# Last expert's part of the first 512 tokens by one-hot products, the other experts' parts combined beside it, MLP weights loaded in halves

## The chip, the cores and the metric

One NeuronCore of one Trainium2 chip runs the whole program; there is no traffic with other cores. The metric is the device time of one execution in microseconds (us). TensorE (PE) multiplies, VectorE (DVE), ScalarE (ACT) and GpSimd (POOL) do elementwise work, SyncE (SP) and POOL issue DMAs; each engine takes its instructions in a fixed order and waits on semaphores.

## The reference, cut to what matters

Two layers on x of shape (2, 1024, 256), fp32. The part around the change is the routed feed-forward of layer 0 and the conditional MLP of layer 1:

```
# L0_ffn: N = 2048 tokens, E = 8 experts, top K = 2, capacity cap = 640 per expert
gates = softmax(top_v)                         # of the two largest logits of a token
exp_batches[e, pos] = x[tok]                   # rows of the tokens that picked expert e
h = exp_batches @ W1;  h = gelu(h_inp) * h_gate;  exp_out = h @ W2
out[tok] = sum over k of gate[tok, k] * exp_out[expert, pos]
x = x + out
# L1_cond, per batch: two picked experts (weighted) and a shared one, hidden width 1024
x1 = sum_e w_e * (gelu(x @ g_e) * (x @ u_e)) @ d_e
```

Layer 0 before it is a conditioned linear layer with causal attention (rotary) and a picked SiLU MLP; layer 1 after it is a minGRU scan, an adapted linear layer and a ternary feed-forward.

## The kernel before, in words

Weights and activations of the large products are split in a high and a low fp32r part, so a product is three matmuls for each 128 of depth: `products` (L932 to L938) issues them at L934, L935 and L936. Tokens stand in the free dimension in 4 chunks of 512 (`CH`), `inH`/`inL` hold the input's two parts, `xT` the residual.

`plan()` writes out by hand the order of the units on every engine (`pe`, `act`, `dve`, `pool`, `sp`); the five programs then walk their lists. A unit's `kind` picks the code, `ready(...)` is the semaphore value at which a unit is done. PSUM banks are handed out in rings (`use`, `bank`), and a matmul waits until what was in its bank has been read.

The experts: `gather` (L1908) fetches 128 rows of an expert's tokens with an indirect DMA, from the scratch `routed_input` in DRAM; `xe` turns them by PE transposes (L1082); `w1` makes 2 halves x 4 blocks x 2 parts of hidden values, with `gelu0` on ACT (L1344), `prod1` on DVE (L1705), `he_hi` on ACT (L1350) and `he_lo` on DVE (L1710); `w2` makes five tiles of output rows, `yrow` copies one to SBUF (L1717) and SP stores it to `expert_output` (L2006). There are four `yrow` buffers, so the copy of tile n waits until the store of tile n - 4 has landed. Beside expert e, `coming_expert(e + 1)` splits the next weights (`wf_hi` L1331 on ACT, `wf_lo` L1907 on POOL) and turns the next rows.

Beside the last expert (7) the first MLP weights are split in 8 pieces: `wm_hi` on ACT (L1369), `wm_lo` on POOL (L1937). They come with one indirect DMA of 3 MB (`ld_mlp`, L1932), issued once the last expert's weights have left the stage buffer. After all 40 output tiles are stored, `fetch` (L1947) gathers for a tile of 128 tokens the two experts' rows, `comb` (L1729, L1731) weighs and adds them, `yt` (L1102) turns the tile, `add` (L1736), `xc_hi` (L1374) and `xc_lo` (L1741) make the MLP's input from it. Four tiles are a chunk. While PE has nothing to do here it runs `spin` matmuls (L950) on constants; their numbers stand in `SPIN`. `early_half` runs the first MLP products (`gu_a`) on the first two tiles of the chunk, so that the products of units 0 to 2 are made in two halves of 256 columns. The other 12 tiles are combined one beside each MLP unit (`combining`).

An MLP unit `gu` is 12 matmuls, followed by `gelu1`, `prod2`, `hm_hi`, `hm_lo`, and two units later `dn` (L1131 to L1133) with 6 matmuls. `split_mlp(1)` splits the second MLP's weights beside units 7 to 14, its low part on DVE (L1722).

```
fetch(0) on POOL: waits for all 40 stores of expert_output and for back_gates
gu(0, 0, 0) on PE: waits for xc_lo of the chunk's last tile and wm_lo(0, 7)
yrow(e, j) on DVE: waits for the store of tile n - 4, then for w2(e, j)
```

Before the experts, routing ends with `inv` (L1074), `slots` (L1334, the token of each slot), then the first gathers, with a spin of 27 matmuls on PE meanwhile; `back_rows`, `back_kept` and `back_gates` on DVE make the rows and gates for the way back.

## Time and profile before

| | |
|---|---|
| median of 3 runs | 999.74 us (998.01 to 1001.44) |
| profiled execution | 1008.6 us |
| its span | 1007.4 us, granted TensorE clock 0.993 in the mean |
| PE busy | 953.5 us (95%) |
| DVE / ACT / POOL busy | 497.4 / 436.1 / 272.2 us |
| moved by DMA | 67.48 MB, mean 67 GB/s |

The profiled execution stands 8.9 us over the median of the runs without a profile. Busy shares are over the whole span; the change touches about 60 us in the middle of it and some 10 us before the experts, so these stretches have to be read by themselves.

### The profile page before, as it was taken

How to read it: one execution, taken by the hardware profiler on the slowest of the kernel's cores; microseconds unless marked ns; L12 is line 12 of the kernel's file. 1: busy time of each engine (PE TensorE's matmuls, PEld its weight loads, DVE VectorE, ACT ScalarE, POOL GpSimd, SP SyncE). 2: the span in 40 equal slices, each digit the busy share in tenths (PEclk: the TensorE clock that was granted, in tenths of full speed). 3: DMA queues.
4: the chain of work that ended last, by engine and by line, in shares of the span. 5: the costliest groups of instructions: out<-in, count | busy, mean ns of one | idle time of the engine just before them, and what ended most of it. 6: DMA issues, size and time to landing. Idle time of an engine off the chain costs nothing.

```text
span 1007.4 us, 13258 instructions
## 1 busy us (share of the span) xinstructions
PE 953.5 (95%) x4952; PEld 783.0 (78%) x4952; DVE 497.4 (49%) x947; ACT 436.1 (43%) x820; POOL 272.2 (27%) x243
## 2 busy tenths in 40 slices
PE   5989999999899999999699999999999999998998
PEld 2667767787589999987587788888888888876786
DVE  5645453566444554544467433333333333688544
ACT  2555564523154444544234334244343342326675
POOL 1333221402256555536452014023041140100000
PEclk9999999999999999999999999999999999999999
DMA  7130001102325444441521300302003003000011
GB/s 261 43 106 21 22 1 64 73 22 84 122 47 125 133 114 133 115 152 35 190 57 39 126 1 1 126 0 110 16 1 126 1 0 126 1 1 1 1 42 43
DMA packets 21648, 67.48 MB, mean 67 GB/s; under 512 B 4497, under 2 KB 11921, under 8 KB 19281
## 3 DMA queue, kind: packets, MB, share of 16 engines
q1 hardware_dynamic: 16592, 39.88, 11.2%
q0 software_dynamic: 4704, 26.49, 9.3%
q8 instruction: 40, 0.66, 0.3%
q10 hardware_dynamic: 288, 0.26, 0.1%
q14 instruction: 24, 0.19, 0.1%
HBM read 55.09 MB, written 9.44 MB: 64 GB/s over the span
## 4 chain that ended last, share of the span: by engine, by line
PE 72%; DVE 12%; ACT 6%; issue 4%; DMA 3%; another core or an unknown queue 1%; SPq 1%; DVEq 0%; ACTq 0%; POOLq 0%
PE banks L934 15%; PE banks L936 14%; PE banks L935 14%; PE banks L1132 4%; PE banks L1133 4%; PE banks L1131 4%; PE banks L1014 3%; PE banks L998 2%; PE banks L1181 1%; PE banks L1180 1%; PE banks L1167 1%; PE banks L1168 1%; PE banks L950 1%; PE banks L1005 1%; DMA expert_output<-y_rows 1%
## 5 line engine op out<-in xcount | busy, mean ns | idle before, releaser
L934 PE MATMUL banks<-input_hi,mlp_hi 128*128 128x512 f32 (+1 forms) x396 | 156.1, 394 | 3.9 <-DVE input_lo L1741 2.4
L936 PE MATMUL banks<-input_hi,mlp_lo 128*128 128x512 f32 (+1 forms) x396 | 155.3, 392 | 0.0
L935 PE MATMUL banks<-input_lo,mlp_hi 128*128 128x512 f32 (+1 forms) x396 | 154.8, 391 | 0.0
L1937 POOL TENSOR_TENSOR mlp_lo<-weight_stage,mlp_hi 128x768 fp32r<-128x768 f32 x40 | 73.6, 1841 | 241.8 <-ACT mlp_hi L1369 241.8
L1384 ACT CAST hidden_hi<-hidden 128x512 fp32r<-128x512 f32 x96 | 59.6, 621 | 176.4 <-DVE hidden L1751 108.0
L1757 DVE TENSOR_TENSOR hidden_lo<-hidden,hidden_hi 128x512 fp32r<-128x512 f32 x96 | 66.5, 693 | 71.3 <-ACT hidden_hi L1384 71.3
L1751 DVE SCALAR_TENSOR_TENSOR hidden<-banks,L_expert_weight,gelu 128x512 f32<-128x512 f32 x64 | 48.0, 751 | 97.6 <-PE banks L936 97.4
L1907 POOL TENSOR_TENSOR ffn_w_lo<-weight_stage,ffn_w_hi 128x512 fp32r<-128x512 f32 x48 | 62.0, 1294 | 109.2 <-ACT ffn_w_hi L1331 109.2
L934 PEld LDWEIGHTS banks<-input_hi,mlp_hi 128*128 128x128 f32 x396 | 75.2, 190 | 20.2 <-issue 4.3
L936 PEld LDWEIGHTS banks<-input_hi,mlp_lo 128*128 128x128 f32 x396 | 75.3, 190 | 16.4
L935 PEld LDWEIGHTS banks<-input_lo,mlp_hi 128*128 128x128 f32 x396 | 75.5, 191 | 16.0
L934 PE MATMUL banks<-expert_in_hi,ffn_w_hi 128*128 128x320 f32 x256 | 82.0, 320 | 3.4 <-DVE hidden L1705 1.8
L1378 ACT ACTIVATE gelu<-banks 128x512 f32<-128x512 f32 x96 | 57.3, 596 | 62.7 <-PE banks L936 62.3
L935 PE MATMUL banks<-expert_in_lo,ffn_w_hi 128*128 128x320 f32 x256 | 80.2, 313 | 0.0
L936 PE MATMUL banks<-expert_in_hi,ffn_w_lo 128*128 128x320 f32 x256 | 80.2, 313 | 0.0
L1132 PE MATMUL banks<-hidden_lo,mlp_hi 128*128 128x512 f32 x192 | 75.4, 392 | 0.0
L1131 PE MATMUL banks<-hidden_hi,mlp_hi 128*128 128x512 f32 x192 | 75.1, 391 | 0.0
L1133 PE MATMUL banks<-hidden_hi,mlp_lo 128*128 128x512 f32 x192 | 75.0, 391 | 0.0
L934 PEld LDWEIGHTS banks<-expert_in_hi,ffn_w_hi 128*128 128x128 f32 x256 | 49.2, 192 | 5.4 <-ACT gelu L1344 2.1
L934 PE MATMUL banks<-ffn_w_hi,expert_hidden_hi 128*128 128x256 f32 x160 | 48.2, 301 | 3.5 <-DVE y_rows L1717 3.0
L1710 DVE TENSOR_TENSOR expert_hidden_lo<-hidden,expert_hidden_hi 128x320 fp32r<-128x320 f32 x64 | 33.9, 530 | 34.0 <-ACT expert_hidden_hi L1350 34.0
L1350 ACT CAST expert_hidden_hi<-hidden 128x320 fp32r<-128x320 f32 x64 | 29.4, 460 | 47.5 <-DVE hidden L1705 47.5
(298 smaller groups left out, 2099.2 us busy)
## 6 DMA issues: line engine op xcount, KB each, us to landing
weight_stage<-in_packF SPq DMA_DIRECT2D x8, 1536.0 KB, 6.9
weight_stage<-in_shared SPq DMA_DIRECT2D x2, 3072.0 KB, 10.9
expert_output<-y_rows SPq DMA_DIRECT2D x40, 128.0 KB
weight_stage<-in_cond_w SPq DMA_DIRECT2D x4, 512.0 KB, 6.4
residual<-in_xT SPq DMA_DIRECT2D x4, 512.0 KB, 10.7
first_half_swapped<-first_half SPq DMA_DIRECT2D x32, 64.0 KB, 2.0
routed_input<-x_rows SPq DMA_DIRECT2D x16, 128.0 KB, 1.8
weight_stage<-in_ffn_w SPq DMA_DIRECT2D x2, 1024.0 KB, 6.8
```

The source lines that it names most:

```text
L934: pe.matmul(o, wh, dh, start=(i == 0), stop=False)
L935: pe.matmul(o, wh, dl, start=False, stop=False)
L936: last = pe.matmul(o, wl, dh, start=False, stop=(i == len(terms) - 1))
L1131: pe.matmul(o, dh[:, i, ms], hiD[r][:, :], start=first, stop=False)
L1132: pe.matmul(o, dh[:, i, ms], loD[r][:, :], start=False, stop=False)
L1133: last = pe.matmul(o, dl[:, i, ms], hiD[r][:, :], start=False, stop=final)
L1378: act.activation(gelu_t[n % 2][:, :], bank(("gu", *key, 0)), ACT.Gelu_apprx_tanh, bias=0.0).then_inc(done)
L1384: act.copy(hiD[n % 4][:, :], prod_t[n % 2][:, :]).then_inc(done)
L1751: dve.scalar_tensor_tensor(prod_t[m % 2][:, :], o, wsel[:, n // 3, n % 3:n % 3 + 1], gelu_t[m % 2][:, :], ALU.mult, ALU.mult).then_inc(done)
L1757: dve.tensor_tensor(loD[m % 4][:, :], prod_t[m % 2][:, :], f(hiD[m % 4][:, :]), ALU.subtract).then_inc(done)
L1907: pool.tensor_tensor(lo, src, f(hi), ALU.subtract).then_inc(done)
L1937: pool.tensor_tensor(wDl[s][:, qs], stage[:, qs], f(wDh[s][:, qs]), ALU.subtract).then_inc(done)
```

## The change

- The output rows of expert 7 for the first 512 tokens no longer go through DRAM. A matrix `hot` (640 slots x 512 tokens, 1 where slot s holds token t) is made by five DVE comparisons beside the `w2` of expert 6. ACT and DVE scale expert 7's output tiles by the slot's gate and split them (`hot_hi`, `hot_lo`), and 20 matmuls of 512 columns sum them straight into the layout of the residual. `hot_add`, `hot_in` and `hot_in_lo` finish the chunk.
- For these tokens `fetch` leaves expert 7 out (its gate is set to 0 and its row to 0), so `fetch`, `comb`, `yt` and `add` of tiles 0 to 3 stand beside expert 7; `fetch` of tile 0 waits for the 35 stores of experts 0 to 6. Tiles 4 to 15 are as before and still wait for all 40, but their steps stand one MLP unit later.
- The gate of each slot of expert 7 is got by way of DRAM: SP writes a table of 2048 gates, one float each, in token order (`gate_table`), and POOL gathers 5 x 128 of them beside expert 2 (`gate_of_slot`). Token numbers count from one, with a row 0 of its own, so that an empty slot is no token's.
- The picked MLP weights are loaded in two halves of 1.5 MB. The first half of MLP 0 is issued beside expert 5, the second where the whole one was; five of the eight split pieces stand beside the `w2` of expert 6, three beside expert 7.
- Gone are the spins of 30 and 7 before the first tiles and the halves of `gu`; a spin of 4 stands before the first `gu`; "slots" goes from 8 to 16, "first rows" from 27 to 13. Some small loads share a semaphore.

POOL from the end of expert 7's weight split on, before (`mlp_lo` is `wm_lo`, `y_first`/`y_second` the fetches of a tile, `in_pack` the MLP load):

```order
L1907 TENSOR_TENSOR ffn_w_lo_173<-weight_stage_52,ffn_w_hi_172 128x512 x2
L1932 DMA weight_stage_52<-in_pack,rows_of_L_cond_63 128x6144
L1937 TENSOR_TENSOR mlp_lo_194<-weight_stage_52,mlp_hi_195 128x768 x8
L1947 DMA y_first_206<-expert_output,route_rows_73 128x256
L1947 DMA y_second_209<-expert_output,route_rows_73 128x256
L1947 DMA y_first_207<-expert_output,route_rows_73 128x256
```

and the same place now:

```order
L2004 TENSOR_TENSOR ffn_w_lo_173<-weight_stage_52,ffn_w_hi_172 128x512 x2
L2035 DMA weight_stage_52<-in_pack_1,rows_of_L_cond_63 128x3072
L2040 TENSOR_TENSOR mlp_lo_202<-weight_stage_52,mlp_hi_203 128x768 x5
L2054 DMA y_first_214<-expert_output,route_rows_73 128x256
L2054 DMA y_second_217<-expert_output,route_rows_73 128x256
L2054 DMA y_first_215<-expert_output,route_rows_73 128x256
L2054 DMA y_second_218<-expert_output,route_rows_73 128x256
L2054 DMA y_first_216<-expert_output,route_rows_73 128x256
L2054 DMA y_second_219<-expert_output,route_rows_73 128x256
L2040 TENSOR_TENSOR mlp_lo_202<-weight_stage_52,mlp_hi_203 128x768
L2054 DMA y_first_214<-expert_output,route_rows_73 128x256
L2054 DMA y_second_217<-expert_output,route_rows_73 128x256
```

Three tiles are now fetched after the fifth piece and the fourth after the sixth. The fourth uses the first one's buffer again, so it waits for that tile's `yt` on PE, and behind it stand two pieces and both halves of MLP 1's load.

DVE at the `w2` of expert 7, now (`last_y_lo` is `hot_lo`, `y_rows` is `yrow`, `residual` is `add` at L1833 and `hot_add` at L1810):

```order
L1806 SCALAR_TENSOR_TENSOR last_y_lo_197<-banks,tiny_71,last_y_hi_196 128x256
L1795 COPY y_rows_187<-banks 128x256
L1806 SCALAR_TENSOR_TENSOR last_y_lo_197<-banks,tiny_71,last_y_hi_196 128x256
L1795 COPY y_rows_188<-banks 128x256
L1833 TENSOR_TENSOR residual_49<-banks,residual_49 128x2x128
L1806 SCALAR_TENSOR_TENSOR last_y_lo_197<-banks,tiny_71,last_y_hi_196 128x256
L1795 COPY y_rows_189<-banks 128x256
L1810 TENSOR_TENSOR residual_49<-banks,residual_49 128x512 x2
L1814 TENSOR_TENSOR input_lo_51<-residual_49,input_hi_50 128x512 x2
```

Where five copies stood alone, each has a `hot_lo` ahead of it, and the chunk's last steps stand behind the last copy, which waits for a store.

The diff, cut to its core:

```
-SPIN = {"first scores": 12, "logits": 5, "slots": 8, "first rows": 27, "first tile": 30, "next tile": 7}
+SPIN = {"first scores": 12, "logits": 5, "slots": 16, "first rows": 13, "first hidden": 4}
...
     def down_expert(e):
         for j in range(ST):
             product("down3", "w2", e, j)
+            if e == G - 1:
+                act.append(("hot_hi", j))
+                dve.append(("hot_lo", j))
             dve.append(("yrow", e, j))
+            if e == G - 2:
+                dve.append(("onehot", j))
+                mlp_piece(j)
...
+    def mlp_piece(q):
+        act.append(("wm_hi", 0, q))
+        pool.append(("wm_lo", 0, q))
+
+    def beside_last_expert():
+        for tt in range(3):
+            pool.append(("fetch", tt))
+        for q in range(ST, PIECES):
+            mlp_piece(q)
+            if q == ST:
+                pool.append(("fetch", 3))
+            yield
+        yield
+        for tt in range(2):
+            dve.append(("comb", tt))
+            yield
+        for tt in range(3):
+            product("turn3", "yt", tt)
+            if tt == 0:
+                dve.append(("comb", 2))
+            dve.append(("add", tt))
+            yield
+        dve.append(("comb", 3))
+        yield
+        yield
+        product("turn3", "yt", 3)
+        dve.append(("add", 3))
+        yield
...
         else:
-            run(weave(expert, split_mlp(0)))
+            run(weave(expert, beside_last_expert()))
...
+    for j in range(ST):
+        pe.append(("hot", j))
+    for k in range(KD):
+        dve.append(("hot_add", k))
+        act.append(("hot_in", k))
+    for k in range(KD):
+        dve.append(("hot_in_lo", k))
+    spin(SPIN["first hidden"], HOT + KD)
...
-    use("first_yt", [(4,), (5,)])
-    for n, _ in enumerate(combine_tiles(0, QT)):
-        if n >= QT // 2 + 1:
-            early_half(n - QT // 2 - 1)
-    pool.append(("ld_mlp", 1))
+    for half in range(2):
+        pool.append(("ld_mlp", 1, half))
...
+            elif kind == "hot":
+                j, = key
+                if j == 0:
+                    for i in range(ST):
+                        pe.wait_ge(*ready("onehot", i))
+                pe.wait_ge(*ready("hot_lo", j))
+                for k in range(KD):
+                    ks = slice(k * P, (k + 1) * P)
+                    pe.matmul(banks[:, HOT + k, :], y7H[:, j, ks], hot[:, j, :], start=(j == 0), stop=False)
+                    last = pe.matmul(banks[:, HOT + k, :], y7L[:, j, ks], hot[:, j, :], start=False, stop=(j == ST - 1))
...
+                dve.tensor_scalar(hot[:, j, :], counting[:, :], slot_number[:, j:j + 1], None, ALU.is_equal).then_inc(done)
...
+            elif kind == "gate_of_slot":
+                pool.iota(counting[:, :], [[1, CH]], base=1, channel_multiplier=0, allow_small_or_imprecise_dtypes=True).then_inc(ramps)
+                pool.wait_ge(ld["gate_table"], 16)
+                for j in range(ST):
...
-                pool.indirect_dma_start(stage[:, 0:PK1], None, A["pack1"], bass.IndirectOffsetOnAxis(ap=dyn1[:, m:m + 1], axis=0)).then_inc(ld["picked_mlp"], 16)
+                pool.indirect_dma_start(stage[:, half * PK1 // 2:(half + 1) * PK1 // 2], None, A[f"pack1_{half}"], bass.IndirectOffsetOnAxis(ap=dyn1[:, m:m + 1], axis=0)).then_inc(ld[f"picked_mlp{half}"], 16)
...
+        sp.wait_ge(*ready("back_gates"))
+        sp.dma_start(gate_rows[1:1 + N, :].rearrange("(n p) a -> p (n a)", p=P), last_gate, allow_slow_non_contiguous=True).then_inc(ld["gate_table"], 16)
```

## Rows read from the trace of the kernel before

**Rows 1.** The page: busy times, and the chain that ended last by engine
```profile
PE 953.5 (95%) x4952; PEld 783.0 (78%) x4952; DVE 497.4 (49%) x947; ACT 436.1 (43%) x820; POOL 272.2 (27%) x243
...
PE 72%; DVE 12%; ACT 6%; issue 4%; DMA 3%; another core or an unknown queue 1%; SPq 1%; DVEq 0%; ACTq 0%; POOLq 0%
```

**Rows 2.** Timeline of PE: start, length, then the idle time before in brackets
```profile
441.60 0.36 PE L934 MATMUL banks<-ffn_w_hi,expert_hidden_hi 128*128 128x256 f32 x1
...
444.43 0.28 PE L936 MATMUL banks<-ffn_w_hi,expert_hidden_lo 128*128 128x256 f32 x1
444.55 0.31 PE L934 MATMUL banks<-expert_in_hi,ffn_w_hi 128*128 128x320 f32 x1
...
448.81 0.31 PE L936 MATMUL banks<-expert_in_hi,ffn_w_lo 128*128 128x320 f32 x1
...
472.08 6.65 PE L950 MATMUL banks<-earlier_token,identity_bf 128*128 128x512 bf16 x30
...
495.39 0.35 PE L934 MATMUL banks<-input_hi,mlp_hi 128*128 128x256 f32 x1 [2.38 <-DVE input_lo L1741]
...
699.79 0.39 PE L935 MATMUL banks<-input_lo,mlp_hi 128*128 128x512 f32 x1
...
704.91 0.39 PE L1133 MATMUL banks<-hidden_hi,mlp_lo 128*128 128x512 f32 x1
```

**Rows 3.** Windows: busy of PE, PEld, DVE, ACT, POOL, granted clock, DMA share, GB/s
```profile
472.00:484.60 12.60, 9.26 (x44) 3.91 (x43) 3.85 (x10) 0.81 (x2) 7.12 (x8) 1.00 0.30 87
484.60:495.40 10.80, 5.12 (x41) 4.78 (x41) 3.11 (x8) 1.41 (x3) 6.35 (x7) 1.00 0.83 315
495.40:500.00 4.60, 4.60 (x26) 4.60 (x27) 1.44 (x2) 2.40 (x4) 0.95 (x1) 0.63 0.67 166
```

**Rows 4.** The chain that ended last, 439 to 479: start, length, what
```profile
439.85 10.17 DMA expert_output<-y_rows
...
475.35 2.82 DMA y_first<-expert_output,route_rows
```

**Rows 5.** Timeline of POOL
```profile
437.65 0.96 POOL L1932 DMA_INDIRECT weight_stage<-in_pack,rows_of_L_cond  x1 [0.81 <-POOL ffn_w_lo L1907]
...
476.61 0.95 POOL L1947 DMA_INDIRECT y_second<-expert_output,route_rows  x1 [0.30 <-issue]
```

**Rows 6.** Timeline of ACT and of DVE beside expert 7
```profile
452.05 0.43 ACT L1344 ACTIVATE gelu<-banks 128x320 f32<-128x320 f32 x1
...
454.19 0.43 ACT L1344 ACTIVATE gelu<-banks 128x320 f32<-128x320 f32 x1
...
450.04 0.42 DVE L1717 COPY y_rows<-banks 128x256 f32<-128x256 f32 x1 [6.24 <-DMA expert_output<-y_rows]
```

**Rows 7.** Groups by line and form: xcount | busy us, mean ns | idle before
```profile
L1937 POOL TENSOR_TENSOR mlp_lo<-weight_stage,mlp_hi 128x768 fp32r<-128x768 f32 x40 | 73.6, 1841 | 241.8 <-ACT mlp_hi L1369 241.8
...
L1563 DVE TENSOR_TENSOR residual<-banks,residual 128x512 f32<-128x512 f32 x8 | 5.5, 692 | 8.0 <-PE banks L936 8.0
L1796 DVE TENSOR_SCALAR below_minus_half<-weight_stage,tiny 128x512 f32<-128x512 f32 x8 | 3.9, 484 | 0.2
...
L1384 ACT CAST hidden_hi<-hidden 128x512 fp32r<-128x512 f32 x96 | 59.6, 621 | 176.4 <-DVE hidden L1751 108.0 <-DVE hidden L1753 68.5
```

**Rows 8.** Timeline of PE and POOL before the first expert
```profile
269.51 1.07 PE L1074 MATMUL banks<-token_at_column,at_low 128*128 128x40 f32 x8 [2.01 <-DVE token_at_column L1651]
270.43 7.69 PE L950 MATMUL banks<-earlier_token,identity_bf 128*128 128x512 bf16 x27
...
280.66 0.38 PE L934 MATMUL banks<-expert_in_hi,ffn_w_hi 128*128 128x320 f32 x1 [0.97 <-issue]
...
273.59 0.94 POOL L1918 DMA_INDIRECT gathered<-routed_input,token_of_slot  x1 [0.30 <-issue]
```

**Rows 9.** DMA queues from 276 to 284: packets, MB, share of 16 engines
```profile
q0 software_dynamic: 315, 0.84, 61.0%
```

**Rows 10.** DMA issues of the whole span: KB each, us to landing
```profile
weight_stage<-in_cond_rep SPq DMA_DIRECT2D x1, 1.0 KB, 2.8
```

186 lines of the change are left out of this document (121 added, 65 removed).

## The prediction

> **What bounds the kernel now.** The page first: PE is busy 95% of the span and makes 72% of the chain that ended last [rows 1], so the kernel is a stream of matmuls, and time can only be won where that stream stops or crawls. The windows by stage show where: between 472.0 and 495.4 us PE's busy time is made of constants' products, transposes and half-width products, with few real columns [rows 3]. The timeline of PE gives the edges of that hole: the last `w2` ends at 472.08, where 30 spins begin, and the first product that needs the whole chunk starts at 495.39 [rows 2]. The chain says what fills it: a store, a gather that takes 2.82 us from issue to landing, and the elementwise steps behind it [rows 4]. A second weak place stands ahead of it: at 439.85 a store of output rows takes 10.17 us, since the 3 MB load was issued at 437.65, and DVE sits idle 6.24 us for it [rows 4, 5, 6]. A third is the wait for the first gathers, which a spin of 27 covers from 270.43 to 278.1, before the first expert product at 280.66 [rows 8].
>
> **The hole before the MLP, before.** Of the first three units' 36 products, the left halves were made inside the hole. Full-width products follow each other by (704.91 - 699.79) / 22 = 0.233 us, 256-wide ones by (444.43 - 441.60) / 24, about 0.119 [rows 2]. Had all been left to do at the end of the hole, it would have cost 36 x (0.233 - 0.119) = 4.1 us more, so the hole's end is worth 495.39 - 4.1 = 491.3.
>
> **The same stretch after the change.** I count from the first `w1` product of expert 7 at 444.55, which the change leaves about where it is.
> - 96 products of `w1` by (448.81 - 444.55) / 29 = 0.147 us [rows 2]: 14.1. Before, a unit took 454.19 - 452.05 = 2.14 us, since ACT had a split piece in each, and DVE had come 6.24 us late [rows 6]. Now three pieces stand here, not eight, and PE is up to two units ahead of them, so PE's own pace counts.
> - four pairs of transposes, 0.3 each: 1.2. They are moved in here, with comb and add, from the hole and hide nothing.
> - 60 products of `w2` by 0.119: 7.2.
> - 20 one-hot products of 512 columns by 0.233: 4.7. The last tile's `hot_hi` and `hot_lo` lie beside the first 16.
> - the tail on the path: `hot_add` 0.69, `hot_in` 0.62, then two `hot_in_lo` of some 0.69 (the row of `hot_add` is the nearest in shape) and the hops [rows 7]: 2.9. The spin of 4 lies inside it.
>
> That is 444.55 + 30.1 = 474.7. I add 1.5 for bank and comb waits (below): 476.2, against 491.3: **-15.1 us**.
>
> What has to hold for it, with what each is behind. The second half load of 1.5 MB is issued at the old place; as 3 MB held the store for 10.17 us, half of it should hold one about 5, so the store issued at 439.85 lands near 445, when the copy that waits for it was due (450.04 less 6.24 is 443.8). The five `wm_lo` of 1.84 us beside `w2` of expert 6 [rows 7] take POOL from about 440 to 450; the three fetches then take 6 issues of 1.25 us (0.95 and 0.30 [rows 5]) to 457.5 and land by 2.8 later: tile 0 at 455, where its comb stands due, tile 2 at 459, some 0.5 late. The fourth fetch waits behind a piece and `yt` of tile 0 and lands near 464, where its comb is due. PE has some 2 us of banks ahead; so 0 to 4 us may be lost here, and I take 1.5. Five comparisons of 0.48 [rows 7] on DVE and five pieces of ACT's beside `w2` of expert 6 fit in its 1.65 us per tile: nothing, and up to 1 if the POOL pieces slow them.
>
> **The first rows.** The spin of 16 instead of 8 runs up to `inv`, where PE sat idle 2.01 us [rows 8]. The third gather is issued at 273.59 and by 2.82 to land is there at 276.4 [rows 4, 8]; at the DMA load of that stretch I say 276.9, and transposes and split add 1.4: first `w1` at 278.3, not 280.66. **-2.3 us.** Here the gate table comes in: five small DVE operations later than the old gates, SP writes 2048 single floats, near 275.5, beside gathers 3 to 5. No row shows such a write. From below, a load of 128 rows of 8 bytes lands in 2.8 us [rows 10]: nothing is lost, and 278.3 stands. From above, gathers of 0.84 MB took 61% of 16 engines over 8 us, 78 us of engines [rows 9], 0.095 for each 1 KB row; 2048 elements at that price are 12 us on 16 engines, and up to that the gathers could come late. An element is nearer to the small row, and the later gathers have 4 us of slack: I take 0 and keep -3.5 to +5. In its own sentence, the rule that speaks against this write: the Trainium skill, DMA: Bandwidth & Descriptors, Rules for kernel authors, says that a strided last dimension "lowers to one descriptor per element" and should be rearranged. With it 2048 descriptors are due; without it, if the short runs were merged, the 2.8 us alone; the forecast takes the first count and a small price.
>
> **The rest.** The half load beside expert 5 is 1.5 MB in front of five gathers and beside five stores; by the same halving a store is held some 5 us, just what the fourth-next copy allows: +0.5, bounds 0 to 3. `gate_of_slot` is six POOL instructions in a gap of over 5 us beside expert 2, ahead of pieces with slack: 0. The combined tiles stand one unit later, so one more unit carries a tile and a DVE split piece together: +0.7. The small loads that now share a semaphore have landed long before its waiters: 0.
>
> Sum: -15.1 - 2.3 + 0.5 + 0.7 = **-16.2 us**. Against the profiled execution of 1008.6 that is 992.4; its 8.9 us over the median stay in both, so I put it on the median: 999.74 - 16.2 = **983.5**.
>
> **The rivals.**
> *The loads of MLP 1 take the store's place.* They are issued right behind the last two pieces: 457.5 + 1.84 + 2.5 for the fourth tile's fetches + 2 x 1.84 is near 466. The store of expert 7's first tile comes near 462: `w1` ends at 459.3, its `w2` 1.4 later, then `hot_lo` and the copy. If POOL is 4 us early or that store late, the fifth copy (it waits for that store) sits until 3 MB are in, near 477.5, and `hot_add` stands behind it, though `hot` ended at 471.6. That gives back some 6 us: 990. For it speaks the row of 10.17 us; against it, POOL's work between. The landing of expert 7's stores also feeds tile 4's comb, due near 484 with some 2 us of slack.
> *The wait moves into expert 7.* The store of expert 6's last tile lands late, fetches start 5 us later, and comb in DVE's fixed order holds `prod1`: 5 us back, 988. The half load speaks against it.
> *The gate table goes ahead of the gathers, at a packet's price.* The 315 packets of the gathers took 78 us, 0.25 us each [rows 9]. One packet for each element makes 2048 x 0.25 / 16 = 32 us in which the third gather waits: `w1` of expert 0 starts near 310, +29 in place of -2.3, in all -15.1 + 29 + 1.2 = +15: 1015, slower. It decides from 0.15 us per element on (19 us). Against it: queues share the engines, and the small load of 128 rows. This is the page's rule at its worst price.
> *No gain.* The hole is mended, but DVE or POOL waits in the new places eat it whole, e.g. both first rivals with a clock that falls, as in the windows, where it stood at 0.63 after the hole [rows 3]. Price: 15 us back, 998 to 1000.
>
> **How the numbers follow.** Forecast as summed 0.66; loads 0.13; wait moved 0.10; no gain 0.04; table 0.04; something better, a clock that stays up, 0.03. A measurement of this kernel tells 0.3%, 3 us, from no change. Faster by more than that: 0.92; same 0.04; slower 0.04. The range takes the bounds of the forecast's own waits and both middle rivals: 978 to 991.
>
> **What would show it.** Right: 20 products on `slot_is_of_token` that follow `w2` without a gap; the first MLP product some 30 to 33 us after the first `w1` product of expert 7, where it was 51 with part of the work done; no DVE wait of over 1 us for a store at expert 7's start; the first `w1` at about 278. Wrong: a copy of `y_rows` waiting for a store ahead of `hot_add` (loads); comb waiting for a fetch by several us in expert 7 (moved); gathers landing late beside the table's write (table). If the gain is under 9 us I have missed a wait; if over 22, a second cost of the old order that I took for hidden.

## The result, and the profile after

The changed kernel takes 1014.12 us (median of 4, 1009.2 to 1015.06) against 1000.51 for the kernel before (4 runs): a ratio of 1.0139 with a 95% interval of 1.0117 to 1.0161. It is **slower by some 13.6 us**; the forecast was 16.2 us faster. A later measurement of both kernels on one chip gave a ratio of 1.0126 [1.0104, 1.0148].

The profiled execution of the changed kernel took 1014.09 us with a span of 1012.8. The kernel before's had 1008.6 and 1007.4. The two spans are thus only 5.4 us apart where the medians are 13.6 apart. That is a finding by itself, and the second profile of the kernel before, below, explains it.

The page of the kernel after, its busy times and the chain that ended last, beside [rows 1]:
```profile
PE 950.8 (94%) x4897; PEld 783.9 (77%) x4897; DVE 515.6 (51%) x965; ACT 438.6 (43%) x823; POOL 282.1 (28%) x253
...
PE 70%; DVE 13%; ACT 7%; issue 5%; DMA 4%; SPq 1%; POOL 0%; DVEq 0%; ACTq 0%
```
PE's share of the chain fell from 72 to 70%, and DVE, ACT, issue and DMA took it. The stalls are in four places: ahead of expert 0, and in experts 2, 6 and 7.

**The first rows.** The timeline of PE and the SyncE queue in the kernel after, the place of [rows 8], then the issues from 274 to 290 with KB each and us to landing:
```profile
271.08 2.98 PE L1004 MATMUL banks<-earlier_token,identity_bf 128*128 128x512 bf16 x13
...
275.83 0.41 PE L1136 MATMUL banks<-identity,gathered 128*128 128x128 f32 x2 [0.83 <-DMA gathered<-routed_input,token_of_slot]
289.40 0.66 PE L1136 MATMUL banks<-identity,gathered 128*128 128x128 f32 x2 [13.16 <-DMA gathered<-routed_input,token_of_slot]
...
291.02 0.61 PE L988 MATMUL banks<-expert_in_hi,ffn_w_hi 128*128 128x320 f32 x1 [0.96 <-issue]
...
274.78 0.38 SPq L2109 DMA_DIRECT2D gate_of_last_expert<-tiny  x1
```
```profile
q1 hardware_dynamic: 2064, 0.01, 7.3%
...
gate_of_last_expert<-tiny SPq DMA_DIRECT2D x1, 8.0 KB, 15.9
```
Read the last two lines together. The write of the gate table is 2048 of the 2064 packets of its queue. They carry 0.01 MB and take only 7.3% of the engines' time, yet the write lands 15.9 us after its issue. The third gather, issued 0.5 us before it, is waited for by PE for 13.16 us. The first `w1` product starts at 291.02, not at 280.66 as before, nor at the forecast's 278.3. It takes 0.61 us instead of 0.38: after the idle 13.16 us the granted clock of the next 5 us is 0.50, where the kernel before had 0.66.

**Experts 6 and 7, up to the MLP.** PE's timeline, where [rows 2] stood:
```profile
453.62 0.69 PE L1136 MATMUL banks<-identity,gathered 128*128 128x128 f32 x2 [2.42 <-DVE expert_in_lo L1776]
...
458.20 0.31 PE L988 MATMUL banks<-expert_in_hi,ffn_w_hi 128*128 128x320 f32 x1
...
472.93 0.41 PE L1156 MATMUL banks<-identity,y_first 128*128 128x128 f32 x2 [2.25 <-DVE y_first L1828]
...
481.17 0.69 PE L1156 MATMUL banks<-identity,y_first 128*128 128x128 f32 x2 [2.87 <-DVE residual L1833]
...
493.55 1.04 PE L1004 MATMUL banks<-earlier_token,identity_bf 128*128 128x512 bf16 x4
...
496.56 0.47 PE L988 MATMUL banks<-input_hi,mlp_hi 128*128 128x512 f32 x1 [1.97 <-DVE input_lo L1814]
```
The hole before the MLP is mended: the 20 one-hot products follow `w2` without a gap, and 3 us after them the MLP starts. But from 458.20 to 496.56 it takes 38.36 us and not the 31.65 of the forecast, and waits for DVE of 2.25 and 2.87 us stand in it, and one of 2.42 us ahead of it in expert 6. The windows in [rows 3]'s form show the clock going with them: 0.92 and 0.88, where [rows 3] had 1.00 inside the hole, and then 0.65 behind it, much as [rows 3] had 0.63:
```profile
440.00:476.00 36.00, 31.18 (x206) 30.06 (x205) 26.49 (x43) 18.12 (x39) 24.72 (x19) 0.92 0.27 89
476.00:496.50 20.50, 15.71 (x90) 13.59 (x88) 14.15 (x25) 5.18 (x11) 6.66 (x6) 0.88 0.52 192
496.50:501.10 4.60, 4.54 (x13) 3.67 (x14) 0.06 (x1) 1.08 (x2) 3.38 (x5) 0.65 0.35 86
```
What held DVE is seen in its timeline beside GpSimd's (POOL), the successors of [rows 5, 6]:
```profile
449.37 1.85 DVE L1801 CAST tiny<-token_of_slot 128x5 f32<-128x5 int32 x1
451.25 1.98 DVE L1802 TENSOR_SCALAR slot_is_of_token<-numbers_from_one,tiny 128x512 fp32r<-128x512 f32 x1
...
459.89 0.47 DVE L1802 TENSOR_SCALAR slot_is_of_token<-numbers_from_one,tiny 128x512 fp32r<-128x512 f32 x1
...
469.19 2.81 DVE L1788 TENSOR_TENSOR expert_hidden_lo<-hidden,expert_hidden_hi 128x320 fp32r<-128x320 f32 x1 [0.53 <-ACT expert_hidden_hi L1411]
...
476.12 3.87 DVE L1788 TENSOR_TENSOR expert_hidden_lo<-hidden,expert_hidden_hi 128x320 fp32r<-128x320 f32 x1 [0.52 <-ACT expert_hidden_hi L1411]
```
```profile
449.34 5.57 POOL L2040 TENSOR_TENSOR mlp_lo<-weight_stage,mlp_hi 128x768 fp32r<-128x768 f32 x3 [1.48 <-ACT mlp_hi L1429]
455.53 3.82 POOL L2040 TENSOR_TENSOR mlp_lo<-weight_stage,mlp_hi 128x768 fp32r<-128x768 f32 x2 [0.62 <-ACT mlp_hi L1429]
462.50 0.96 POOL L2054 DMA_INDIRECT y_first<-expert_output,route_rows  x1 [3.15 <-issue]
...
469.81 1.83 POOL L2040 TENSOR_TENSOR mlp_lo<-weight_stage,mlp_hi 128x768 fp32r<-128x768 f32 x1
...
476.04 3.59 POOL L2040 TENSOR_TENSOR mlp_lo<-weight_stage,mlp_hi 128x768 fp32r<-128x768 f32 x2
```
A cast of five numbers takes 1.85 us while GpSimd subtracts, and the one-hot row after it 1.98. The last row, at 459.89 with GpSimd idle, takes 0.47. The two long `hidden_lo` (0.49 otherwise) end at 472.00 and 479.99, each 0.36 us after the end of GpSimd's subtractions (471.64, 479.63).

The two are not alike. The second outlasts a queued pair. The first waits for a single piece, and it starts 0.62 us ahead of it in the profile, while GpSimd is still issuing the last of six loads (468.85 to 469.80); its own 0.49 us would have fitted in. A `hidden_lo` at 467.78, also beside such an issue but with no piece right behind it, took 0.49. Why the first is held before the piece begins is not shown. The cast and the one-hot row are different again: GpSimd's first three pieces end at 451.19, 452.95 and 454.91, the cast ends at 451.22 and the row at 453.23. So these two, each with one tensor as input, got in behind one piece of the row, not behind the last.

**Beside expert 2** a pair holds `hidden_lo` behind the burst of gate loads. GpSimd issues five gathers and five gate loads in a row, the weight pieces queue up behind them, and two then run without a gap, again with `hidden_lo` started 0.66 us ahead of them and ended 0.35 us behind them:
```profile
343.77 3.55 DVE L1788 TENSOR_TENSOR expert_hidden_lo<-hidden,expert_hidden_hi 128x320 fp32r<-128x320 f32 x1 [0.52 <-ACT expert_hidden_hi L1411]
```
```profile
344.43 2.54 POOL L2004 TENSOR_TENSOR ffn_w_lo<-weight_stage,ffn_w_hi 128x512 fp32r<-128x512 f32 x2
```

### The profile page after: what moved, and what is told of

The parts are those of the page before. It is cut to its first block, busy times and chain, and to the rows that moved or that the text cites. A ratio compares the mean times of both kernels' runs of the same rounds, so it can differ in the third digit from the quotient of the medians.

```text
span 1012.8 us, 13193 instructions
## 1 busy us (share of the span) xinstructions
PE 950.8 (94%) x4897; PEld 783.9 (77%) x4897; DVE 515.6 (51%) x965; ACT 438.6 (43%) x823; POOL 282.1 (28%) x253
## 4 chain that ended last, share of the span: by engine, by line
PE 70%; DVE 13%; ACT 7%; issue 5%; DMA 4%; SPq 1%; POOL 0%; DVEq 0%; ACTq 0%
PE banks L988 14%; PE banks L990 14%; PE banks L989 14%; PE banks L1193 4%; PE banks L1192 4%; PE banks L1194 4%; PE banks L1068 3%; PE banks L1052 2%; DMA gathered<-routed_input,token_of_slot 1%; PE banks L1242 1%; PE banks L1241 1%; DVE hidden L1783 1%; PE banks L1228 1%; PE banks L1229 1%; PE banks L1059 1%
## 5 line engine op out<-in xcount | busy, mean ns | idle before, releaser
L988 PE MATMUL banks<-input_hi,mlp_hi 128*128 128x512 f32 x384 | 153.9, 401 | 2.0 <-DVE input_lo L1814 2.0
L990 PE MATMUL banks<-input_hi,mlp_lo 128*128 128x512 f32 x384 | 153.2, 399 | 0.0
L989 PE MATMUL banks<-input_lo,mlp_hi 128*128 128x512 f32 x384 | 152.5, 397 | 0.0
L988 PEld LDWEIGHTS banks<-input_hi,mlp_hi 128*128 128x128 f32 x384 | 72.5, 189 | 18.9 <-issue 2.4
L990 PEld LDWEIGHTS banks<-input_hi,mlp_lo 128*128 128x128 f32 x384 | 72.5, 189 | 17.2
L989 PEld LDWEIGHTS banks<-input_lo,mlp_hi 128*128 128x128 f32 x384 | 72.9, 190 | 16.6
L1788 DVE TENSOR_TENSOR expert_hidden_lo<-hidden,expert_hidden_hi 128x320 fp32r<-128x320 f32 x64 | 40.3, 629 | 34.0 <-ACT expert_hidden_hi L1411 34.0
L2016 POOL DMA_INDIRECT gathered<-routed_input,token_of_slot x40 | 39.2, 980 | 41.0 <-ACT token_of_slot L1395 17.7
```

What stands on the lines that cost most here:

```text
L988: pe.matmul(o, wh, dh, start=(i == 0), stop=False)
L989: pe.matmul(o, wh, dl, start=False, stop=False)
L990: last = pe.matmul(o, wl, dh, start=False, stop=(i == len(terms) - 1))
```

## The theories

A: the table's write of single elements holds up the gathers. B: GpSimd's subtractions, queued back to back, hold up DVE operations that read two tiles of SBUF or a wide one. C: the burst of indirect loads beside expert 2 makes such a queue. D: the first profile of the kernel before had stalls that a typical execution lacks, and the forecast counted them as gain. E: the shorter filler ahead of expert 0 costs clock. The rivals stand in the expectations. The experiments ran on four chips, and each ratio is to the kernel before on the same chip, whose medians were 1006.0 for the first four runs below, 999.4 for the next four, 998.8 for the next four and 1009.8 for the last three.

## Experiments on the gate table

**The write moved behind expert 0's stores.**
```
-        sp.wait_ge(*ready("back_gates"))
-        sp.dma_start(gate_rows[1:1 + N, :]..., last_gate, ...)
         for e in range(G):
...
                 sp.dma_start(rows_out[n * P:(n + 1) * P, :], yrow[n % 4][:, :])...
+            if e == 0:
+                sp.wait_ge(*ready("back_gates"))
+                sp.dma_start(gate_rows[1:1 + N, :]..., last_gate, ...)
```


> The changed kernel with one move: SyncE issues the write of the gate table (2048 single floats) after the five stores of expert 0 instead of ahead of them. Theory A (the write, 15.9 us from issue to landing in the changed kernel's profile, holds back the third to fifth gather, whose transposes waited 13.2 us for them): the first w1 product starts at 278 to 279 us instead of 291.0, and the time falls by 11 to 13 us, to 1001 to 1003. Rival A2 (the delay is the lower granted clock and the shorter filler, and the gathers would be late without the table too): first w1 at 289 or later, time within 2 us of 1014. Rival A3 (the write harms wherever it stands): what is won at expert 0 is lost at the gathers or the weight load of experts 1 to 3, and the time falls by less than 5 us.

**The same write added to the kernel before.** Nothing reads it there.
```
+        sp.wait_ge(*ready("back_gates"))
+        sp.dma_start(gate_rows[1:1 + N, :].rearrange("(n p) a -> p (n a)", p=P), gates[:, 0:2, :, :]..., ...)
         for e in range(G):
```


> The kernel before with one addition: a write of 128x16 floats as 2048 single elements to a table in memory, issued by SyncE at the same place as in the change; nothing reads the table. Theory A: the first w1 product moves from 280.66 us to 291 to 294, and the time rises by 10 to 12 us, to 1010 to 1013. Rival A2: first w1 within 1 us of 280.7, time unchanged.

**The same bytes in 128 runs.** The gates of expert 7's slots come out permuted.
```
-        sp.dma_start(gate_rows[1:1 + N, :].rearrange("(n p) a -> p (n a)", p=P), last_gate, ...
+        sp.dma_start(gate_rows[1:1 + N, :].rearrange("(p n) a -> p (n a)", p=P), last_gate, ...
```


> The changed kernel with the gate table written at the same place, but with the 16 floats of a partition next to each other in memory: 128 runs of 64 B instead of 2048 of 4 B (the gates of the last expert are then looked up in the wrong order; the work is the same). Theory A in the form that the number of separate elements is what costs: the write lands in under 4 us, the first w1 product starts at 278 to 280, the time falls by 11 to 13 us, as with the write moved. If it is the wait or the place on the queue that costs, not the elements: first w1 stays near 291 and the time near 1014.

Measured: moved 0.9999 [0.9977, 1.0021]; added to the kernel before 1.0063 [1.0045, 1.0080]; in 128 runs 0.9989 [0.9968, 1.0010]. PE's timelines show the third transposes and the first `w1` product. With the write moved:
```profile
280.51 0.41 PE L1136 MATMUL banks<-identity,gathered 128*128 128x128 f32 x2 [1.65 <-DMA gathered<-routed_input,token_of_slot]
281.89 0.38 PE L988 MATMUL banks<-expert_in_hi,ffn_w_hi 128*128 128x320 f32 x1 [0.97 <-issue]
```
Added to the kernel before:
```profile
291.68 0.66 PE L1083 MATMUL banks<-identity,gathered 128*128 128x128 f32 x2 [7.75 <-DMA gathered<-routed_input,token_of_slot]
293.31 0.61 PE L935 MATMUL banks<-expert_in_hi,ffn_w_hi 128*128 128x320 f32 x1 [0.97 <-issue]
```
In 128 runs:
```profile
277.70 0.41 PE L1136 MATMUL banks<-identity,gathered 128*128 128x128 f32 x2 [2.06 <-DMA gathered<-routed_input,token_of_slot]
279.08 0.60 PE L988 MATMUL banks<-expert_in_hi,ffn_w_hi 128*128 128x320 f32 x1 [0.97 <-issue]
```
The start of this stretch moves by up to 4 us between profiles, so count from the first product of the token counts in each: 26.6 us to `w1` after the change, 14.9 with the write moved, 15.3 in runs, 25.9 with the write in the kernel before. Theory A holds in its form of element count: the same 8 KB at the same place cost nothing in 128 pieces and 11 us in 2048. (The profile gives no landing time for the write in 128 pieces, so the expected "under 4 us" is not shown.) Moved behind the stores, the write still took 14.1 us to land, but nobody waited. Two misses: the time gained was 1.3 to 1.5% rather than the 1.1 to 1.3 expected (by ratios from different chips), and added to the kernel before the write cost 6 us, not 10 to 12. There part of the late start came back, from the first `w1` product of expert 0 to that of expert 7: 160.8 us against 163.9 in the first profile. That profile has three stalls of 3.7 to 4.2 us of ScalarE in this stretch, and the one with the write has none; whether that is the write's doing is not shown.

## Experiments on GpSimd's queue

**One-hot rows and last pieces spread over expert 7.** `ONEHOTS` is the hidden steps 0 to 4.
```
             if e == G - 2:
-                dve.append(("onehot", j))
                 mlp_piece(j)
...
                 dve.append(("he_lo", e, h, i))
+                if e == G - 1 and h * IT + i in ONEHOTS:
+                    dve.append(("onehot", ONEHOTS.index(h * IT + i)))
...
     def mlp_piece(q):
         act.append(("wm_hi", 0, q))
-        pool.append(("wm_lo", 0, q))
+        if q < ST:
+            pool.append(("wm_lo", 0, q))
+        else:
+            dve.append(("wm_lo_dve", 0, q))
```


> The changed kernel with two moves beside expert 7: the five one-hot rows are made in its first five hidden steps instead of in expert 6's down products, and the last three pieces of the MLP weights' low parts are subtracted by VectorE instead of GpSimd. Theory B (GpSimd's subtractions, once they stand queued back to back, hold up VectorE's operations that read two SBUF tiles or a wide one: 2.81 and 3.87 us instead of 0.49 for a hidden_lo, 1.4 to 2.0 instead of 0.47 for a one-hot row; this makes PE's waits of 2.42, 2.25 and 2.87 us): no hidden_lo above 1 us in expert 7, first MLP product 31 to 34 us after the first w1 of expert 7 instead of 38.4, and the time falls by 6 to 10 us, to 1004 to 1008. Rival B2 (the waits come from the late fetches, held by expert 6's last store, whatever VectorE does): the waits stay, time within 2 us of 1014. Rival B3 (VectorE is full: the subtractions cost it 3 x 0.96 us): the gain is under 4 us.

Measured: 1.0048 [1.0027, 1.0069], so 0.8 to 0.9% under the changed kernel's ratio, as theory B said (6 to 10 us). The one-hot rows take 0.48 us in the mean. The longest `hidden_lo` is 1.21 (expected: none over 1), beside a piece of GpSimd's. PE's waits of 2.42, 2.25 and 2.87 us are gone, with others of 0.2 to 1.14 in their place. From `w1` of expert 7 to the MLP it takes 35.6 us (expected 31 to 34): better than 38.4, not what was forecast.

**Both edits together:** the diff of the moved table and that of the spread.

> The changed kernel with both edits: the table written after expert 0's stores, and one-hot rows and the last three pieces of the low parts spread over VectorE in expert 7. If the two costs are separate they add: table -1.4% (ratio 0.9999 against 1.0139), spread -0.9% (1.0048 against 1.0139), so a ratio to the kernel before of 0.989 to 0.994, some 6 to 11 us faster than the kernel before. If they hide one another (a delay at expert 0 that comes back as less waiting later), the ratio is 0.996 or more.

**The pieces alone.** The table moved, and of the spread's diff only the part on `mlp_piece`; the one-hot rows stay in expert 6.

> The changed kernel with the table write moved and the last three pieces on VectorE, but the one-hot rows left in expert 6's down products, beside GpSimd's subtractions. Theory B: one-hot rows still take 1.4 to 2.0 us and PE still waits about 2.4 us for expert_in_lo there, while in expert 7 no hidden_lo takes over 1.3 us; the time lies 2 to 5 us above the kernel with both edits and 4 to 7 below that with the table alone moved. If VectorE's one-hot rows are slow by themselves (not by GpSimd), nothing of this tells; if it is expert 7's one-hot rows that cost, this kernel is no slower than the kernel with both edits.

Measured: both 0.9956 [0.9939, 0.9973], pieces alone 0.9963 [0.9950, 0.9976]. The costs do not add in full: 0.4% beyond the table's repair, where 0.9 was expected. The ratio lies between the two expectations, so the chips or a delay that hides another took half; which is open. With pieces alone the one-hot rows stay slow, the groups of DVE by form (count, then busy us and mean ns) saying
```profile
L1807 DVE TENSOR_SCALAR slot_is_of_token<-numbers_from_one,tiny 128x512 fp32r<-128x512 f32 x5 | 7.9, 1580 | 0.0
```
and in the kernel with both edits
```profile
L1809 DVE TENSOR_SCALAR slot_is_of_token<-numbers_from_one,tiny 128x512 fp32r<-128x512 f32 x5 | 2.4, 482 | 0.0
```
but PE waits 0.7 us for it, not 2.4, and the difference in time is 0.7 us (expected 2 to 5), inside the intervals. So the rows are slow because of GpSimd, and what that costs depends on how GpSimd's pieces fall against them.

**The burst beside expert 4.**
```
-            if e == 2:
+            if e == 4:
                 pool.append(("gate_of_slot",))
```


> As the kernel with both edits, with the burst of five gate loads by GpSimd (in a row with the five gathers) beside expert 4 instead of expert 2. In the profiles with the table moved, written in rows, or with the spread, ScalarE stood still for 9.0 us at the first gelu of expert 2, beside that burst, PE waited 3.7 us and expert 2 took 28.2 to 28.6 us from its first product to the next expert's, against 22.4 for experts 4 to 6. Theory C (the burst of ten indirect loads makes it): the stall moves to expert 4, which then takes 26 to 28 us, and expert 2 takes 24 or less; time within 2 us of the kernel with both edits. Rival C2 (it belongs to expert 2 whatever is loaded there, as the stalls of 3.7 to 4.2 us of the kernel before do): it stays at expert 2. Rival C3 (it takes the burst and something that only expert 2 has): it is gone at both, and 3 to 6 us are won.

Measured: 0.9958 [0.9940, 0.9977], as with the burst at expert 2. The 9.0 us stall of ScalarE on which the expectation was built did not occur on this chip, in any version. What the burst does by itself is smaller and moves with it. In the kernel with both edits expert 2 took 25.11 us and expert 4 22.35; here expert 2 took 22.56 and expert 4 24.84, with the long `hidden_lo` again 0.35 us behind GpSimd's queued pair:
```profile
379.24 3.55 DVE L1795 TENSOR_TENSOR expert_hidden_lo<-hidden,expert_hidden_hi 128x320 fp32r<-128x320 f32 x1 [0.53 <-ACT expert_hidden_hi L1418]
```
```profile
379.88 2.56 POOL L2011 TENSOR_TENSOR ffn_w_lo<-weight_stage,ffn_w_hi 128x512 fp32r<-128x512 f32 x2
```
**One gate load per expert,** and the one-hot rows at steps 3 to 7 instead of 0 to 4.
```
-            if e == 2:
-                pool.append(("gate_of_slot",))
+            if e >= 2:
+                pool.append(("gate_of_slot", e - 2))
```

> As the kernel with both edits, with one gate load behind the gathers of each of experts 2 to 6 instead of five beside expert 2, and the one-hot rows at hidden steps 3 to 7 of expert 7, beside no subtraction of VectorE's. Theory C: no stall over 5 us on ScalarE in any expert, every expert from 1 on within 22.3 to 24.6 us, and a time 4 to 6 us below the kernel with both edits (some 12 to 16 us below the kernel before). Rivals C2, C3: within 2 us of the kernel with both edits.

> The same kernel as the best so far (table write later, one gate load per expert, one-hot rows and last pieces on VectorE in expert 7), beside the changed kernel on one chip: ratio 0.991 to 0.995 to the kernel before, as the first time (0.993), so 2.0 to 2.3% below the changed kernel. If the ratio of the changed kernel came from its chip or day, the two are closer.

Measured: 0.9930 [0.9914, 0.9946], and on a second chip 0.9929 [0.9908, 0.9951], 1.9% under the changed kernel beside it (expected 2.0 to 2.3): 7 us **faster than the kernel before**, 2.6 us under both edits (expected 4 to 6, with a stall in it that this chip did not have). Experts 1 to 5 take 22.35 to 22.56 us each. Theory C holds at 2.5 us for the burst by these profiles: expert 2 went from 25.11 to 22.55 us. The time alone would not show it, as the intervals overlap and the one-hot rows moved in the same step. No run separates the loads from the pair of pieces queued behind them.

**GpSimd keeps the pieces, ahead of the fetches.** `mlp_piece` is as in the changed kernel again, the rest as in the best so far (the table write later, the gate loads apart, the one-hot rows at steps 3 to 7).
```
-        for tt in range(3):
-            pool.append(("fetch", tt))
         for q in range(ST, PIECES):
             mlp_piece(q)
-            if q == ST:
-                pool.append(("fetch", 3))
+            if q == PIECES - 1:
+                for tt in range(4):
+                    pool.append(("fetch", tt))
             yield
```


> As the best so far, but the last three pieces of the low parts are GpSimd's again, and stand ahead of the fetches in its order instead of between them. Theory B (what costs is that subtractions stand queued back to back, not that GpSimd does them): each runs as ScalarE hands it over, with VectorE's hidden_lo in the gaps at 0.8 to 0.9 us as in the kernel before, none above 1.3 us; but the fetches start about 5 us later, so PE waits 1 to 4 us for y_first; time 0 to 4 us above the best. Rival B4 (GpSimd's subtractions cost VectorE the same wherever they stand): hidden_lo of 2 us and more, and a time 4 to 8 us above the best.

Measured: 0.9944 [0.9925, 0.9963], with an interval that overlaps that of the best so far (0.9929). The same three subtractions on the same engine now run singly, and DVE fits between them, as in these lines of DVE and of POOL:
```profile
447.12 0.84 DVE L1789 TENSOR_TENSOR expert_hidden_lo<-hidden,expert_hidden_hi 128x320 fp32r<-128x320 f32 x1 [0.53 <-ACT expert_hidden_hi L1412]
```
```profile
443.62 1.91 POOL L2042 TENSOR_TENSOR mlp_lo<-weight_stage,mlp_hi 128x768 fp32r<-128x768 f32 x1 [0.16 <-ACT mlp_hi L1430]
445.76 1.85 POOL L2042 TENSOR_TENSOR mlp_lo<-weight_stage,mlp_hi 128x768 fp32r<-128x768 f32 x1 [0.23 <-ACT mlp_hi L1430]
```
No `hidden_lo` is over 1.05 us. Its fetches are later, and PE waits 2.47 us for `y_first`, as expected. Rival B4 falls: what costs is not who subtracts, but when the piece starts. Here each starts when ACT hands it over (GpSimd idles 0.16 and 0.23 us before it), and `hidden_lo` starts only some 0.5 us before its end. In the changed kernel a piece stood ready behind the loads and started where `hidden_lo` was due.

Theory B stands in a narrower form than it was put. Over the 17 profiles 52 `hidden_lo` took longer than 0.52 us, and each ended 0.34 to 0.36 us after a GpSimd subtraction. In nine of them two subtractions ran without a gap, and all nine (3.55 to 3.87 us) ended behind the second. But one alone made 2.81 us too, so the queue of two is the worst case and not the condition.

## The kernel before, profiled again

> The kernel before, unchanged, for a second profiled execution. Its first one took 1008.6 us, 8.9 over the median, and it shows stalls of 2.6 to 4.2 us on ScalarE, VectorE and GpSimd that no tile or transfer explains: three at expert boundaries, three inside the hole before the MLP. Theory D (these stalls are what lies over the median, so part of the hole that the forecast counted as taken away is not there in a typical execution): a profile near the median shows no or few of them, 158 to 161 us from the first w1 product of expert 0 to that of expert 7 instead of 163.9, and 42 to 45 us from there to the start of the unbroken MLP products, less the early ones, instead of 46.7. Rival D2 (the excess lies before the experts, or after the hole): both stretches are within 1 us of the first profile.

> The changed kernel, unchanged, on the same chip as the kernel before: ratio 1.010 to 1.016, as the first measurement (1.0139). In the profile: the third gather's transposes 11 to 14 us late, a hidden_lo of VectorE of 2.8 and one of 3.9 us in expert 7.

Measured: the kernel before 1.0003 [0.9989, 1.0016] to itself, its new profile 997.15 us with a span of 995.9; the changed kernel 1.0126, span 1010.7. The waits that the profile lays to no tile, in the first profile of the kernel before:
```profile
ACT expert_in_hi L1340 <- remote: 11.5, 3, 4.2
DVE residual L1736 <- remote: 6.5, 2, 3.6
DVE y_rows L1717 <- remote: 2.7, 1, 2.7
POOL y_first L1947 <- remote: 2.6, 1, 2.6
```
(engine, what waited, us in total, times, longest). The new profile has **none** of them. In that of the changed kernel the third transposes wait 11.87 us and the two long `hidden_lo` take 2.47 and 3.85, about as expected. The landmarks of the two new profiles, on one chip; first the kernel before:
```profile
272.14 6.00 PE L950 MATMUL banks<-earlier_token,identity_bf 128*128 128x512 bf16 x27
...
280.68 0.38 PE L934 MATMUL banks<-expert_in_hi,ffn_w_hi 128*128 128x320 f32 x1 [0.97 <-issue]
...
438.16 0.31 PE L934 MATMUL banks<-expert_in_hi,ffn_w_hi 128*128 128x320 f32 x1
```
and the changed kernel:
```profile
290.74 0.60 PE L988 MATMUL banks<-expert_in_hi,ffn_w_hi 128*128 128x320 f32 x1 [0.96 <-issue]
...
458.06 0.31 PE L988 MATMUL banks<-expert_in_hi,ffn_w_hi 128*128 128x320 f32 x1
...
495.98 0.47 PE L988 MATMUL banks<-input_hi,mlp_hi 128*128 128x512 f32 x1 [1.97 <-DVE input_lo L1814]
```
From expert 0's first `w1` product to expert 7's the kernel before takes 157.48 us, not 163.89 (expected 158 to 161); from there to the end of its span 557.7, not 1007.4 - 444.55 = 562.9. So 5.1 us of the last stretch, and 6.4 of the one ahead of it, were in the first profile alone, with its stalls and the lower clock behind them (0.63 after the hole in [rows 3], 1.00 here), and theory D holds. They go with the chip: on the two chips where the kernel before took 1006 and 1010 us, six of the seven profiles show waits of this kind over 2 us on ScalarE between 255 and 515 us, and the seventh on DVE; on the two where it took 999, none of eight shows any there. Which chip gave the first profile is not on record; its runs without a profile took 998 to 1001 us.

The two profiles give the account of the change on a chip without these stalls, in us:

| stretch | before | changed | difference |
|---|---|---|---|
| token counts to first `w1` product | 15.23 | 25.44 | +10.2 |
| expert 0 | 22.77 | 25.43 | +2.7 |
| expert 2 | 22.55 | 25.10 | +2.6 |
| expert 6 | 22.35 | 27.32 | +5.0 |
| experts 1, 3, 4, 5 | 89.81 | 89.47 | -0.3 |
| expert 7's first `w1` to the end | 557.74 | 552.64 | -5.1 |

An expert counts from its first `w1` product to the next one's. The sum is 14.95, and the changed kernel came to the token counts 0.15 earlier: the difference of the spans, 14.8.

## Experiments on the filler

> The kernel before with the changed kernel's two filler counts ahead of the first expert (16 and 13 instead of 8 and 27), nothing else. The forecast's second term made this -2.3 us. Theory E: the first w1 starts at most 0.5 to 2.5 us earlier after the count products, expert 0 takes 1.5 to 2.5 us longer at a lower clock, and the time is 0 to 2 us longer. As forecast: 2 to 3 us shorter.

> The best so far with one number changed: 27 filler products ahead of the first gathered rows, as in the kernel before, instead of 13. Theory E (the shorter filler lets PE stand idle in three gaps of 0.6 to 2 us, the granted clock falls, and the first products of expert 0 run at half speed: expert 0 takes 24.2 to 25.5 us against 22.8 in the kernel before's typical profile, more than the earlier start wins): the first w1 product still starts within 1 us of 15 us after the count products, expert 0 takes 22.8 us, and the time falls by 1 to 3 us, a ratio of 0.990 to 0.992. Rival E2 (the filler delays the transposes by what it lengthens): the first w1 starts 1.5 to 3 us later, and the time stays within 1 us.

> As the kernel with 27 filler products, and 11 instead of 4 fillers between the one-hot products and the MLP. There PE stood idle for 1.98 us, and its clock was 0.66 in the first 5 us of the MLP. Theory E: the clock stays at 1.0 through the first 5 us, which wins 1 to 2 us more. Rival: the fillers end later than the input's low part and cost as much as they win, within 0.5 us.

The edits, first in the kernel before, then in the best so far (the second experiment has the first of its numbers alone, the third both):
```
-SPIN = {"first scores": 12, "logits": 5, "slots": 8, "first rows": 27, ...
+SPIN = {"first scores": 12, "logits": 5, "slots": 16, "first rows": 13, ...
```
```
-SPIN = {..., "slots": 16, "first rows": 13, "first hidden": 4}
+SPIN = {..., "slots": 16, "first rows": 27, "first hidden": 11}
```

Measured: the kernel before with the short filler 0.9999 [0.9984, 1.0015]. The forecast said -2.3 us for it, and theory E 0 to +2: nothing can be measured. Its `w1` starts 14.96 us after the counts against 16.93 in the first profile (15.23 in the undisturbed one), and the granted clock over the next 24 us is 0.87 against 0.93 there, in the windows of the two (first the kernel before, then with the short filler):
```profile
280.70:304.70 24.00, 24.00 (x167) 23.95 (x168) 11.72 (x26) 12.23 (x29) 12.62 (x12) 0.93 0.15 45
```
```profile
278.70:302.70 24.00, 23.99 (x157) 23.95 (x157) 10.88 (x25) 12.04 (x28) 13.62 (x12) 0.87 0.18 52
```
Ten products fewer in the same 24 us: expert 0 takes 25.6 us instead of 24.3, and gives back two thirds of the earlier start.

The new profile of the kernel before shows why there was so little to win. Its 27 fillers take 6.00 us, at a clock of 1.00, and the same 27 took 7.69 in the first profile [rows 8], at 0.78. The forecast thus counted 1.7 us of slow filler as time that a shorter filler saves. Of `w1`'s start only 0.3 to 0.4 us was there to win (15.23 against 14.88 in the best so far on the same chip). There expert 0 then takes 24.2 us at a clock of 0.93 over 24 us, against 22.8 at 1.00. That speaks for theory E, in one profile each.

With 27 fillers put back the ratio is 0.9905 [0.9886, 0.9924], with 11 fillers ahead of the MLP as well 0.9894 [0.9874, 0.9913]. These are 2.5 and 3.6 us under the version that they start from, on another chip; the intervals overlap in each of the two steps, so neither is shown. Both together lie just clear of the starting version, but the chips differ in more than the filler: here the kernel before has its stalls in the hole, and they go with the hole. From expert 7's start to the end the kernel before with the short filler takes 562.95 us and the version with 27 fillers 552.64, where the fast chip has 557.7 and 552.5. That alone can make the gain. Expert 0 took 25.1 and 24.3 us, not the expected 22.8; this chip has the stalls, and the first profile of the kernel before, with them, had 24.3 too. At the MLP's start these two profiles differ as expected, in the windows of its first 5 us, first with 4 fillers, then with 11:
```profile
484.00:489.00 5.00, 4.83 (x14) 3.85 (x15) 0.16 (x2) 1.19 (x2) 3.78 (x5) 0.66 0.39 105
```
```profile
483.00:488.00 5.00, 4.96 (x21) 4.07 (x22) 1.13 (x2) 2.09 (x4) 3.56 (x4) 1.00 0.40 98
```
21 products instead of 14 at 1.00 of the clock instead of 0.66 (2.4 GHz throughout, against part of the time at 1.2), after an idle gap of 0.46 us instead of 1.98. But the same can be had without the edit. The second profile of the changed kernel, with 4 fillers and an idle gap of 1.97 us, shows
```profile
495.90:500.90 5.00, 4.92 (x21) 4.04 (x22) 1.09 (x2) 2.10 (x4) 3.78 (x5) 1.00 0.39 102
```
Of the twelve profiles with 4 fillers, eight have 0.66 in these 5 us and four have 1.00. One profile with 11 does not show that the filler made the difference. This last version beats the kernel before on its chip, 998.6 us to 1009.8, most of it by the edits ahead of this section.

## Why the prediction was wrong

1. *"I take 0 and keep -3.5 to +5"* for the gate table: **the step that failed most**. The working had two ends, 0 by the load of 128 small rows [rows 10] and 12 us by the price of a gathered row [rows 9], and took the lower since "an element is nearer to the small row". It measured 10.2 us on one chip, and 11.3 against the write in 128 runs, near the upper end. The row of [rows 10] has 128 pieces, the write 2048; it was like in size and unlike in count, and count was the cost. The range was then cut at +5, which neither end supports. The rule cited with it, that such a dimension becomes one descriptor per element, is what the trace shows (with the write alone added, packets under 512 B rose from 4497 to 6560), and its advice, to rearrange, is what the third experiment did. The rival *gate table ahead of the gathers* had the place right and the price too high: 32 us for 15.9, since the elements took 7.3% of the engines' time and not all of it. Its sign was the one that came, at a chance of 0.04. That its total of 1015 is 1 us from the measured 1014 is luck: its table is some 20 us too dear, and its hole gains 10 us too much, with the losses in experts 0, 2 and 6 not in it.
2. *The hole, -15.1 us.* Measured from expert 7's start to the end of the span it is -5.1 (forecast -15.1 + 0.7 for the combined tiles there). The mechanism was right: products on `slot_is_of_token` without a gap, PE's first full product at once behind the tail, a tail of 3.0 us where 2.9 was said. The size was off in two places. Of the 46.7 us that the old stretch was credited with, some 5 were stalls, and the clock behind them, of the profiled execution (5.1 to the end of the span): the step *"its 8.9 us over the median stay in both"* failed. And the new stretch overran by 6.3 to 6.7 (37.9 and 38.4 us for 31.65), by the waits for DVE of 2.25 and 2.87 us and the clock that fell behind them; of this, 2.1 came back after the MLP's start on the chip without stalls. The profiles show part of it: there the kernel before waits 1.35 us for DVE's `y_first` at 491.74, in the MLP's first units, and the changed kernel has no such wait. The rest is open.
3. *"nothing, and up to 1 if the POOL pieces slow them"* for the five comparisons beside expert 6, priced at 0.48 us each [rows 7]: they took 1.42 in the mean, and expert 6 lost 5.0 us on the chip without stalls, of which 2.44 are PE's wait and part is the clock, 0.91 in the 18 us around it. GpSimd was named as the risk and its size was not looked for. In the kernel before `hidden_lo` already took 0.81 to 0.86 us beside each of GpSimd's single pieces; that they would stand ready behind the fetches, once ACT runs ahead, could have been read from the order of work.
4. *`gate_of_slot`: 0.* It was 2.5 us, by a pair of pieces queued behind the loads: six instructions fit into GpSimd's gap by time, but not ahead of the pieces that ACT had ready.
5. *First rows, -2.3:* 0 measured. The term was read from a profile whose 27 fillers took 7.69 us instead of 6.00, so 0.3 to 0.4 was there to win. The sum also has no term for the clock: expert 0 took 2.7 us longer (0.88 over its first 24 us), behind the short filler and the idle 11.87 us of the late gather. The other terms were small and did little: a store did hold a copy of DVE 3.39 us behind the half load, but PE shows no wait for it (+0.5 forecast), and PE waits 0.52 us for a combined tile at 562.66 in the changed kernel's second profile (+0.7 forecast).
6. *The rivals.* The wait did move into expert 7, but not by late fetches as that rival had it: the y rows were there when DVE came late. The loads of MLP 1 did make a copy of `y_rows` wait 2.16 us ahead of `hot_add`, which then still waited 0.98 for PE, so it cost nothing. "Under 9 us I have missed a wait" was the sign that fired.

The engine pair that contends is what the Trainium skill says, SBUF — State Buffer, Who interferes with whom: a VectorE instruction with two SBUF inputs, or in a two-port mode, and a GpSimd instruction that reads SBUF block each other, and issue order decides who waits. The trace agrees for single pieces: a `hidden_lo` that starts beside one ends 0.35 us after it, whether that makes 0.84 us or 2.81. It goes further where two subtractions follow without a gap: in all nine such cases VectorE's operation with two inputs ended 0.36 us after the second, not after the first. With one piece of 1.84 us [rows 7] and these 0.35, an estimate by the page is at most 2.2 us, where 2.81 and 3.87 came.

## What to carry to other kernels

Price a DMA by the number of separate pieces, and put one with thousands of them where no gather stands behind it. Before work is put on an engine in a gap, ask what will be queued behind it when it ends: here a GpSimd subtraction held a VectorE operation with two SBUF inputs until it had ended, and two in a row held it until the second had. Let each wait for its own input rather than stand ready behind a row of loads. And take a profile that lies 9 us over the median for what it is: compare every stretch that you mean to remove with a second profile before you count it as gain.

## What was not expected of the hardware

- 2048 elements of 4 B took 10.3 to 15.9 us to land (5 to 8 ns each), at 7.3% of the engines' time, and held gathers on another queue meanwhile; in 128 runs of 64 B the same 8 KB held nothing. Why the gathers wait while the engines are mostly idle is not shown here.
- VectorE's wait behind GpSimd, for operations with two SBUF inputs, spans two instructions that follow each other without a gap (3.87 us for two of 1.8), with 0.35 us to the end of its own operation. It can begin 0.6 us ahead of the subtraction, while GpSimd still issues loads.
- A cast of five numbers per partition took 1.85 us beside a GpSimd subtraction of the same length, and ended 0.03 us after it: small size did not help it. It did not wait for the next two, which followed without a gap.
- Chips differ by 1% on this kernel (999 against 1006 and 1010). Profiles from the slower two show stalls of 2 to 9 us on ScalarE, VectorE and GpSimd that the profile lays to no tile, and those from the faster show none. What they are was not tried. The longest, 9.0 us at expert 2's first gelu, was seen in three kernels on one chip, each with the gate loads beside it, and never on the two fast chips.
